# Query norms in half-width column groups, and their factor applied with the subtraction of the maximum

## The reference

```python
def rmsnorm(x, g, eps=EPS):
    var = jnp.mean(jnp.square(x), axis=-1, keepdims=True)
    return x * jax.lax.rsqrt(var + eps) * g
q = (hidden_states @ Wq).reshape(B, Sq, H, D)
k = (encoder_hidden_states @ Wk).reshape(B, Skv, H, D)
q = rmsnorm(q, gq)
k = rmsnorm(k, gk)
scores = jnp.einsum('bqhd,bkhd->bhqk', q, k) * scale
attn = jax.nn.softmax(scores, axis=-1)
```

## Time and profile before

| | |
|---|---|
| time, median of 3 runs | 731.33 us (729.55 to 734.58) |
| the profiled execution | 731.66 us, of which 729.6 are the span from the first to the last instruction |
| mean granted TensorE clock | 0.995 of full speed |
| TensorE busy | 708.9 us, 97% of the span |
| VectorE busy | 478.0, 66% |
| ScalarE busy | 378.9, 52% |
| GpSimd busy | 317.5, 44% |
| stage a | from about 20 to about 252 us of the span |

### The profile page before, as it was taken

One profiled execution on the slowest core, in us unless ns is written; L12 is line 12 of the kernel. 1 busy time (PEld: TensorE's weight loads), 2 busy tenths in 40 slices (PEclk: granted clock), 3 DMA queues, 4 the chain that ended last, 5 costly groups with the idle time before them and its releaser, 6 DMA issues.

```text
span 729.6 us, 15412 instructions
## 1 busy us (share of the span) xinstructions
PE 708.9 (97%) x5242; PEld 627.2 (86%) x5242; DVE 478.0 (66%) x1065; ACT 378.9 (52%) x840; POOL 317.5 (44%) x404
## 2 busy tenths in 40 slices
PE   7999999999999899999999999999999999999997
PEld 5899998899988789888898889888888888888886
DVE  4565658665585666668776677886555788655555
ACT  3677777677777433434443543335345744444442
POOL 3444433444444333433333424443545476555553
PEclk9999999999999999999999999999999999999999
DMA  8112121101000012121222111210332322323322
GB/s 283 45 44 65 45 63 56 34 23 32 25 31 12 30 39 78 59 77 58 59 68 85 59 58 60 78 59 24 88 105 88 85 76 81 107 86 94 101 86 86
DMA packets 35690, 49.85 MB, mean 68 GB/s; under 512 B 3904, under 2 KB 22720, under 8 KB 35648
## 3 DMA queue, kind: packets, MB, share of 16 engines
q1 hardware_dynamic: 35648, 49.29, 22.5%
HBM read 48.22 MB, written 1.05 MB: 68 GB/s over the span
## 4 chain that ended last, share of the span: by engine, by line
PE 73%; DVE 15%; ACT 5%; issue 3%; DMA 2%; POOL 1%; SPq 1%; DVEq 0%
PE acc L479 17%; PE bank_q L437 13%; PE bank_k L437 11%; PE bank_p L603 7%; PE bank_v L536 4%; PE bank_s L579 4%; PE bank_s L437 4%; PE bank_v L437 4%; PE bank_v L551 3%; DMA raw_b<-in_head_b 2%; PE bank_s L564 2%; PE bank_t L587 1%; DVE sc_sub L1053 1%; DVE hh L1124 1%; DVE pv_lo L1034 1%
## 5 line engine op out<-in xcount | busy, mean ns | idle before, releaser
L479 PE MATMUL acc<-wo_hi,pv_hi 128*128 128x256 f32 x328 | 93.5, 285 | 2.8 <-DVE pv_lo L1034 1.5
L479 PE MATMUL acc<-wo_hi,pv_lo 128*128 128x256 f32 x328 | 92.6, 282 | 0.0
L479 PE MATMUL acc<-wo_lo,pv_hi 128*128 128x256 f32 x328 | 91.9, 280 | 0.0
L1227 POOL TENSOR_TENSOR wq_lo<-raw_b,wq_hi 128x256 fp32r<-128x256 f32 x32 | 24.1, 754 | 145.8 <-DVE wq_hi L1080 145.8
L1227 POOL TENSOR_TENSOR sq_k_lo<-sq_k,sq_k_hi 128x512 fp32r<-128x512 f32 x32 | 41.3, 1291 | 78.3 <-ACT sq_k_hi L784 78.3
L437 PE MATMUL bank_q<-xt_hi,wq_hi 128*128 128x512 f32 x178 | 74.1, 416 | 0.0
L1034 DVE TENSOR_TENSOR pv_lo<-bank_p,pv_hi 128x512 fp32r<-128x512 f32 x64 | 43.9, 686 | 44.7 <-ACT pv_hi L818 44.7
L1227 POOL TENSOR_TENSOR wq_lo<-raw_m,wq_hi 128x256 fp32r<-128x256 f32 x50 | 43.6, 871 | 65.7 <-DVE wq_hi L1083 65.7
L437 PE MATMUL bank_q<-xt_lo,wq_hi 128*128 128x512 f32 x178 | 70.7, 397 | 0.0
L437 PE MATMUL bank_q<-xt_hi,wq_lo 128*128 128x512 f32 x178 | 70.6, 397 | 0.0
L479 PEld LDWEIGHTS acc<-wo_hi,pv_hi 128*128 128x128 f32 x328 | 61.7, 188 | 7.7 <-DVE pv_lo L1034 2.9
(11 more groups left out here) (192 smaller groups left out, 2111.5 us busy)
## 6 DMA issues: line engine op xcount, KB each, us to landing
raw_m<-in_chunk_m SPq DMA_DIRECT2D x50, 256.0 KB, 2.7
raw_a<-in_head_a SPq DMA_DIRECT2D x48, 192.0 KB, 2.4
raw_b<-in_head_b SPq DMA_DIRECT2D x32, 256.0 KB, 2.8
raw_m<-in_chunk_m SPq DMA_DIRECT2D x50, 128.0 KB, 2.0
raw_v<-in_pair_v SPq DMA_DIRECT2D x16, 256.0 KB, 2.8
raw_b<-in_head_b SPq DMA_DIRECT2D x32, 128.0 KB, 2.0
xs<-in_x SPq DMA_DIRECT2D x8, 128.0 KB, 3.7
out<-xs SPq DMA_DIRECT2D x4, 256.0 KB, 2.3
```

Source lines behind the costliest of these rows:

```text
L479: last = nc.tensor.matmul(acc[t // 2][:, (t % 2) * D:(t % 2 + 1) * D], w[:, tok], m, start=False, stop=True, skip_group_check=True)
L1227: nc.gpsimd.tensor_tensor(lo, raw, hi, ALU.subtract).then_inc(signal, 1)
```

## The change

On TensorE, norm_q takes 64 tokens at a time instead of 128, in eight products, and puts each into the half of the partitions where its sequence stands, as scores does. The sum of the logs on GpSimd goes. ScalarE makes two roots instead of one: r_k (128 x 256) from ln_k and r_q (128 x 4) from ln_q, both before vo_hi. VectorE multiplies the scores by r_k alone; the subtraction of the maximum, one operation of 128 x 256, becomes four of 128 x 64 with two factors for each partition: minus the maximum, times r_q. Stage b keeps the one subtraction.

```diff
             def norm_q(u):
                 pe.wait_ge(A["sq_q"], u.done())
-                for t in range(NT):
-                    last = nc.tensor.matmul(bank_v[:, D + t:D + t + 1], sq_q[:, t * P:(t + 1) * P], ones[:],
-                                            start=True, stop=True)
+                for b in range(NS):
+                    t, s = divmod(b, SPB)
+                    last = nc.tensor.matmul(bank_v[s * SEQ:(s + 1) * SEQ, D + t:D + t + 1],
+                                            sq_q[:, b * SEQ:(b + 1) * SEQ], ones[:], start=True, stop=True)
...
-            def roots(u):
-
-                act_e.wait_ge(A["ln_qk"], u.done())
-                nc.scalar.activation(r_qk[:], ln_qk[:], ACT.Exp, scale=-0.5).then_inc(A["r_qk"], 1)
+            def root_k(u):
+
+                act_e.wait_ge(A["ln_k"], u.done())
+                nc.scalar.activation(r_k[:], ln_k[:], ACT.Exp, scale=-0.5).then_inc(A["r_k"], 1)
+
+            def root_q(u):
+
+                act_e.wait_ge(A["ln_q"], u.done())
+                nc.scalar.activation(r_q[:], ln_q[:], ACT.Exp, scale=-0.5).then_inc(A["r_q"], 1)
...
                 if nxt.kind == "a":
+                    root_k(nxt)
                     log_q(nxt)
+                    root_q(nxt)
...
-                if nxt.kind == "a":
-                    roots(nxt)
...
                 if u.kind == "a":
-                    v.wait_ge(A["r_qk"], u.done())
+                    v.wait_ge(A["r_k"], u.done())
...
-                    nc.vector.tensor_tensor(sc[:], found, r_qk[:], ALU.mult).then_inc(A["scaled"], 1)
+                    nc.vector.tensor_tensor(sc[:], found, r_k[:], ALU.mult).then_inc(A["scaled"], 1)
...
                 v.wait_ge(stage["max"], u.done())
-                nc.vector.tensor_tensor(sc_sub[:], sc[:], sc_max[:].unsqueeze(2).to_broadcast([P, NT, SEQ]),
-                                        ALU.subtract).then_inc(stage["sub"], 1)
+                if u.kind == "a":
+                    v.wait_ge(A["r_q"], u.done())
+                    for t in range(NT):
+                        under = nc.vector.tensor_scalar(sc_sub[:, t, :], sc[:, t, :], sc_max[:, t:t + 1], r_q[:, t:t + 1],
+                                                        ALU.subtract, ALU.mult)
+                else:
+                    under = nc.vector.tensor_tensor(sc_sub[:], sc[:], sc_max[:].unsqueeze(2).to_broadcast([P, NT, SEQ]),
+                                                    ALU.subtract)
+                under.then_inc(stage["sub"], 1)
...
-            def add_logs(u):
-                pool.wait_ge(A["ln_k"], u.done())
-                pool.wait_ge(A["ln_q"], u.done())
-                nc.gpsimd.tensor_tensor(ln_qk[:], ln_k[:], ln_q[:].unsqueeze(2).to_broadcast([P, NT, SEQ]), ALU.add)\
-                    .then_inc(A["ln_qk"], 1)
```

More of the change, by code:

```diff
@@ L238, in flamingo_layer @@
         ln_k, ln_q = sb("ln_k", [P, NT, SEQ]), sb("ln_q", [P, NT])
-        ln_qk, r_qk = sb("ln_qk", [P, NT, SEQ]), sb("r_qk", [P, NT, SEQ])
+        r_k, r_q = sb("r_k", [P, NT, SEQ]), sb("r_q", [P, NT])
         sc = sb("sc", [P, NT, SEQ])
@@ L285, in flamingo_layer @@
                        "sub exp sum inv norm t_done attn_t_lo attn_t vo_done vo_hi vo_lo ssk_done ssq_done ln_q "
-                       "ln_k ln_qk r_qk pv_done pv_hi pv_lo wo_done")
+                       "ln_k r_k r_q pv_done pv_hi pv_lo wo_done")
         B = stage_sems("b", "wq_hi wq_lo wk_hi wk_lo wv_hi wv_lo wo_hi wo_lo q_done k_done v_done qt kt vs scores scaled max sub exp sum inv norm t_done attn_t_lo attn_t "
@@ L923, in _ @@
             log_k(start)
-            roots(start)
+            root_q(start)
+            root_k(start)
             split_context(1)
@@ L1279, in head @@
                 split_second(after)
-                if nxt.kind == "a":
-                    add_logs(nxt)
                 if u.kind == "b":
@@ L1318, in _ @@
             split_second(start.next())
-            add_logs(start)
             split_context(1)
```

## The result

The changed kernel takes 752.52 us (median of 4 runs, 751.29 to 753.73), the kernel before 732.96 beside it (median of 4, 729.55 to 737.05). The ratio is 1.0263, 95% interval 1.0227 to 1.0298: slower, by 19.6 us. The profiled execution took 753.73, with a span of 751.6 against 729.6.

What follows compares the result with a forecast made beforehand. It took TensorE, busy 97% but only just ahead of the other engines, as decisive. Losses in both halves, three late heads and half 1's beginning, less the first two norm_q, gave +20.9 on 731.3: 752, range 737 to 759.

Steps and rivals of the forecast that it cites:

- both halves collide: Cross attention: subtractions in both halves are held by GpSimd's sq_k_lo; 752 us, chance 0.57.
- Half 1 stays clear: Rival: with a subtraction step under 0.21, half 1 gains 0.26 per head and only half 0 collides; 740 us, chance 0.20.
- No collision at all: Rival: 64-column VectorE operations are not held by GpSimd in either half; 730 us, no change, chance 0.08.
- Faster: Rival: TensorE's saving arrives, the subtraction group being through by V + 3.07 in both halves; 723 us, chance 0.07.
- norm_q: TensorE, each cross-attention head: half-width norm_q takes 0.57 until scores instead of 0.99, saving 0.42, not all of it arriving.
- V can move by 0.26 at most: V, the first weight load of the attention values, waits for ScalarE's attn_t, so at most 0.26 per head arrives.
- ScalarE in half 0: Roots ahead of vo_hi delay pv_lo to V + 2.39, 0.18 later than now, in a head otherwise 0.26 earlier.
- Half 0: First 16 heads of the cross attention: the second subtraction is held, +0.8 per head, 14 passes, 11.2 in all.
- Half 1: Last 16 heads of the cross attention: the fourth subtraction is held, period 7.46 for 6.73, 12 passes, 8.6 in all.
- Three late heads: Heads where token preparation already delays the subtraction: +0.45 each, two giving back 0.42 through norm_q, +0.5 in all.
- The beginning of half 1: Where half 1 begins, VectorE reads the accumulators behind the attention, 1.4 later.
- First two norm_q: The first two norm_q of the cross attention, which nothing else holds, save 0.84.

Runs made afterwards that it cites:

- e3: The changed kernel with three subtractions instead of four, the third taking 128 columns; 739.24 us, ratio 1.0130 to the kernel before.
- e5: The changed kernel with GpSimd starting sq_k_lo only when the head's subtraction is done; 734.99 us, ratio 1.0058 to the kernel before.
- e6: The kernel before with only the subtraction split into four, the second factor a column of ones; 762.93 us, ratio 1.0410.
- e9: The changed kernel with vo_hi ahead of the roots and two whole 256-column operations, subtraction then product with r_q; 726.69 us, ratio 0.9900 to the kernel before.
- e2: The changed kernel with the full-width norm_q put back; 760.86 us, ratio 1.0426 to the kernel before.
- e10: The changed kernel with vo_hi ahead of the roots, r_k times r_q before the scaling and one subtraction; 725.95 us, ratio 0.9912 to the kernel before.
- e1: The kernel before with the half-width norm_q alone; 726.88 us, ratio 0.9933.
- e11: The changed kernel with vo_hi ahead of the roots and two whole operations, run once more; 727.35 us, ratio 0.9932 to the kernel before.
- e13: The changed kernel, vo_hi ahead of the roots, two whole operations in half 0, early product of factors in half 1; 723.04 us, ratio 0.9860 to the kernel before.

## Why the prediction was right

**The mechanism.** The likeliest case came in: both halves collide, at 752.5 for 752. The fourth operation of half 1 started at V + 3.10 and sq_k_lo at V + 3.07, as read from the earlier trace rows; e3, e5, e6 and e9 show from four sides that this is the loss and not something that goes along with it. "Half 1 stays clear" needed a step under 0.21; it is 0.22, as extrapolated from the earlier trace rows, and a single operation takes 0.30 to 0.31. The prediction set 0.32 against a formula's 0.19 and put the difference down to the two factors; but a copy of 256 columns, which has none, takes 0.28, so of the 0.41 only about 0.13 can be theirs. "No collision at all" fell: operations of 64 columns are held too. "Faster" asked for a group that is through by V + 3.07 in both halves. No kernel here is the changed one with just that; e9 comes nearest, with a last operation that starts by then and ends at V + 3.31, and takes 726.7 where the rival said 723. In its profiled execution the 14 passes of half 0 give 0.22 each of the 0.26, and the settled ones of half 1 0.14, since GpSimd pays there; the pass from head 16, in which the granted clock was 0.50, is 0.80 longer than before.

**The terms of the sum.**

- *norm_q.* Predicted 0.57 to scores and 0.42 saved. Measured 0.57 in the row above, 0.46 in most heads, so up to 0.52 saved there; but the change of width now falls between the turn and norm_q and costs 0.20 there (last section). From the turn to scores, like compared with like, it is 0.83 against 1.16 (e2) where TensorE waited before the turn, and 0.89 against 1.20 (e3, before) where it did not: 0.33 or 0.31 saved. This is the term that was mis-sized: the change of width was left out. The estimate that V can move by 0.26 at most, bound by attn_t, held only where pv_lo was in time: e3 and e10 reach 6.50 in half 1, 0.22 less than before, and 6.47 in a plain head, 0.26 less. With the other parts of before it was 0.11 in half 1 (e1), for r_qk, and that was not in the prediction.
- *ScalarE in half 0.* Predicted pv_lo at V + 2.39, measured 2.33 to 2.45, in one head 2.20. Predicted group from V + 2.99, end 4.87, turn 6.51; in the head shown V + 2.93, 4.87 and 6.49. Of the settled heads 1 to 12 four have the first operation held instead of the second (group end 5.05 to 5.07, turn 6.68 to 6.70) and take longer.
- *Half 0.* 14 x 0.8 = 11.2 predicted, 11.53 measured.
- *Half 1.* 7.46 predicted, 7.47 to 7.49 in a plain head; +8.6 for 12 heads predicted, +10.15 for 13 passes measured. The prediction's terms cover 30 of the 31 passes; the one left out, at its own price, is 0.72 of the difference. What was mis-sized besides: 7.61 in the heads where scores begin late behind norm_q, and two passes at +0.98 and +0.99 (from 25, where the group starts at V + 2.67 and ends at 4.64, and from 16, where the clock is low).
- *Three late heads.* +0.5 predicted, +0.60 measured.
- *The beginning of half 1.* +1.4 predicted, +2.11 measured. The turn ahead of it was 1.58 later, at V + 6.47 instead of 4.89, because there the group starts at V + 2.80 and already the second operation, at V + 3.02, is held. The rest goes with the clock, below: from the turn to the next V it takes 3.85, against 3.35 in e10, where the granted clock stayed at 1.00.
- *First two norm_q.* -0.84 predicted, -1.53 at the first V. This term was not shown: the first V stands at 26.84 in e9 and at 28.50 in e11, which are the same kernel, so one execution can't resolve it.

That the sum came so close is in part luck. Half 0, half 1, its beginning and the late heads cost 2.7 more than predicted; the first V (-0.7 against its term) and the -0.87 behind the cross attention, which was in no term, took 1.6 of that back. Against the kernel before beside it, at 732.96 and not 731.3, the loss is 19.6 for the predicted 20.9.

## What to carry to other kernels

Before a VectorE operation is split or added, look at which GpSimd operation starts next, and leave a margin for the start of the last operation of the chain: when that started 0.18 ahead of GpSimd's (e9), the chain took its own length and GpSimd's operation 0.1 more; when it started 0.03 behind (the changed kernel), it waited for all of GpSimd's. Not every VectorE operation is held (below), so it matters too which ones stand there. Splitting one 256-column operation into four for the sake of per-partition factors cost 0.56 here where it ran free, and 1.5 where it did not; a second whole operation with a spread factor cost 0.45. When a shared factor is taken apart, place each piece on the engine and at the time where nothing waits, and do so separately for each loop body: the best place differed between the two halves.

## What the runs showed of the hardware

**The hold begins before GpSimd's recorded start.** DVE and POOL in two heads of half 0 of the changed kernel:

```profile
76.95 1.95 DVE L1063 TENSOR_SCALAR sc_sub<-sc,sc_max,r_q 128x64 f32<-128x64 f32 x4
...
93.08 2.08 DVE L1063 TENSOR_SCALAR sc_sub<-sc,sc_max,r_q 128x64 f32<-128x64 f32 x4
...
77.04 1.35 POOL L1241 TENSOR_TENSOR sq_k_lo<-sq_k,sq_k_hi 128x512 fp32r<-128x512 f32 x1 [2.73 <-ACT sq_k_hi L785]
...
93.16 1.28 POOL L1241 TENSOR_TENSOR sq_k_lo<-sq_k,sq_k_hi 128x512 fp32r<-128x512 f32 x1 [2.71 <-ACT sq_k_hi L785]
```

The group that starts 0.09 before sq_k_lo runs its first operation free and is held at its second; the one that starts 0.08 before it is held at its first (which then lasts 1.41). A held operation of 64 columns ends 0.05 behind GpSimd's end. Whole operations on two tensors did not go by this limit: four of them, in e9, e10, e11 and e13, start 0.07 to 0.08 before sq_k_lo and none is held; sq_k_lo takes 1.49 to 1.51 instead. DVE and POOL in head 1 of e9:

```profile
36.72 0.43 DVE L1066 TENSOR_TENSOR sc_sub<-sc_sub,r_q 128x256 f32<-128x256 f32 x1
...
36.79 1.50 POOL L1240 TENSOR_TENSOR sq_k_lo<-sq_k,sq_k_hi 128x512 fp32r<-128x512 f32 x1 [3.05 <-ACT sq_k_hi L785]
```

Where sq_k_lo had to wait, it ended 1.15 behind the end of the VectorE operation that was under way. In a head of half 1 it ended at V + 4.46 instead of 4.36 in e9, where that operation ended at V + 3.31, and was not moved in half 0 of e10, where it ended at V + 3.22. So each waits for the other, and which of the two does is not decided by GpSimd's recorded start but a little ahead of it, by an amount that these runs give only as under 0.1. By the Trainium skill, "Perfetto Trace Analysis", section "GPSIMD Engine Instruction", the engine consists of eight processors and the recorded start is the read request of one of them; that would fit a hold that begins earlier, but no run here shows which processor was first.

**Not every VectorE operation is held.** DVE in the head of the earlier trace rows, where sq_k_lo runs from 161.87 to 163.16:

```profile
162.25 0.42 DVE L1056 TENSOR_REDUCE ex_sum<-ex 128x4 f32<-128x256 f32 x1 [0.48 <-ACT ex L839]
...
162.91 0.53 DVE L1060 TENSOR_TENSOR attn<-ex,ex_inv 128x256 f32<-128x256 f32 x1
```

The sum ex_sum starts 0.38 behind sq_k_lo and takes its usual 0.42, as it did in every other head of these kernels in which it starts while sq_k_lo runs; pv_lo, which reads PSUM, took its usual 0.68 in the nine heads in which it does. Held were the subtractions, with or without factors, and attn (0.53 here, 0.43 in the earlier trace rows). No experiment here separates what decides it.

**Changing the width of the weight tiles costs 0.20.** From the turn (128 columns) to norm_q it took 0.17 in e2, where norm_q has 128 columns, and 0.37 with 64 in the changed kernel; TensorE had waited before the turn in both. Where it had not waited, it was 0.21 and 0.41 (e3). "[0.17 <-issue]" in the row of norm_q is the idle time of the weight loads that comes with it. The rows of e2 (half 1, PEld):

```profile
189.48 0.20 PEld L587 LDWEIGHTS bank_t<-sm,attn 128*128 128x128 f32 x2 [1.08 <-DVE attn L1073]
189.65 0.97 PEld L551 LDWEIGHTS bank_v<-ones,sq_q 128*128 128x128 f32 x8
```

By the Trainium skill, "TensorEngine Tiling (Array Packing)", section "Key Properties", a change of the tiling mode, unlike that of the tile, drains TensorE; the rows agree. Part of it stood behind norm_q before: eight full-width loads step by (0.97 - 0.19) / 7 = 0.11, which makes 0.89, and scores followed after 0.99.

**A wait on VectorE can be paid a second time in TensorE's clock.** Busy times and granted clock (PEclk) of the changed kernel in two stretches at the beginning of half 1:

```profile
150.00:156.00 6.00, 3.56 (x38) 2.82 (x36) 5.38 (x13) 3.73 (x10) 2.42 (x3) 1.00 0.00 0
157.50:159.50 2.00, 2.00 (x13) 1.92 (x10) 0.84 (x2) 0.00 (x0) 0.00 (x0) 0.50 0.09 32
```

The columns are the stretch, its length, the busy time of PE, PEld, DVE, ACT and POOL, PEclk, DMA share and GB/s. TensorE had been busy for 3.56 of 6.00, and its granted clock then fell from 1.00 to 0.50, the 1.2 GHz level, for over 2 us: the eight weight loads of the values take 1.78 there, and 0.97 at 1.00. The same shows in e6_four_alone inside half 1 (the row of 1.72 above), where idle times of 1.3 came in most heads, and three of the 8 passes cost 0.25 to 0.3 more. It is not so in every head that waits: in heads 17 to 25 of the changed kernel TensorE waits 1.05 to 1.29 before each turn, and the granted clock stayed at 1.00; in e2, with waits of 1.06 to 1.08, two of the 8 passes were slowed. The kernel before, in the 6.00 ahead of the same place, was busy for 5.22 and kept 1.00 behind it:

```profile
139.00:145.00 6.00, 5.22 (x42) 4.51 (x43) 4.47 (x11) 4.36 (x10) 3.04 (x4) 1.00 0.02 4
145.00:147.00 2.00, 2.00 (x27) 1.84 (x22) 0.84 (x2) 0.46 (x1) 0.00 (x0) 1.00 0.34 94
```

The kernel before has such a fall too, at 221.2, in a late head. This price of waiting was in no term of the sum.
